# Two graph layers on one core: chunks of 128 edges against windows of 32 nodes, relation products ahead of the gather, and one fused last stage

## The reference, cut to what matters

```python
# layer 0: attention over the edges, 4 heads of 64
enh = x + 0.1 * query_emb
Q, K, V = enh @ Wq + bq, enh @ Wk + bk, enh @ Wv + bv          # [N, 4, 64]
scores = einsum('ehd,ehd->eh', Q[dst], K[src] + 0.2 * rel_w[edge_type_64][:, None]) / 8
w = segment_softmax(scores, dst)
agg = segment_sum(w[:, :, None] * V[src], dst)                 # V itself where a node has no edge
y = layernorm(agg @ Wo + bo + x) * gamma + beta
x = layernorm(x + y)
# layer 1: six relations, then attention of a node's six sums with each other
msgs = (x @ W[r] + b[r])[src]                                  # r = edge_type_6
s = segment_sum(msgs, (dst, r))                                # [N, 6, 256]
q, k, v = split(s @ in_proj_w.T + in_proj_b)
attn = softmax(q k^T / 8) v                                    # 6 x 6, 4 heads
h = (attn @ attn_out_w.T + attn_out_b).mean(over the 6)
x = layernorm(x + (h + x) @ proj_w.T + proj_b)
```

## Time and profile before

| stage | us of the span | TensorE busy | VectorE busy | GpSimd busy | granted clock |
|---|---|---|---|---|---|
| tables | 0 to 230 | 38 | 114 | 60 | 1.00 |
| project | 230 to 427 | 155 | 82 | 66 | 0.96 |
| attend | 427 to 3846 | 2772 | 2895 | 2633 | 0.85 |
| update | 3846 to 4165 | 135 | 168 | 140 | 0.50 |
| relate | 4165 to 7512 | 2047 | 1446 | 1793 | 0.72 |
| mix | 7512 to 9652 | 2069 | 800 | 36 | 0.94 |

### The profile page before, as it was taken

The page is one execution under the profiler, slowest core; times in us unless marked ns, Lnnn a source line. Parts: engine busy times, 40 slices in busy tenths (PEclk is TensorE's granted clock), DMA queues, the critical chain, the costliest instruction groups (busy, mean ns, idle before and its releaser), DMA issues. The chain is left out here.

```text
span 9651.6 us, 171842 instructions
## 1 busy us (share of the span) xinstructions
PE 7214.7 (75%) x38149; PEld 5255.0 (54%) x38149; DVE 5504.5 (57%) x13126; ACT 3186.7 (33%) x13071; POOL 4727.5 (49%) x5036
## 2 busy tenths in 40 slices
PE   1788888888888887446666665666666899999999
PEld 1355555555555554245555555555555566666666
DVE  4488888888888887544444444444444333333333
ACT  0266666666666666100000000000000244433334
POOL 2477777777777776455555555555555000000000
PEclk9888888888888887567777777777777899999989
DMA  2556666666666666233333333333337201111100
GB/s 84 170 184 201 203 203 201 205 202 200 202 202 198 200 201 145 87 95 92 93 92 92 92 90 91 91 95 91 92 93 80 61 28 36 36 36 37 35 27 25
DMA packets 480675, 1131.97 MB, mean 117 GB/s; under 512 B 86354, under 2 KB 280648, under 8 KB 466304
## 3 DMA queue, kind: packets, MB, share of 16 engines
q0 software_dynamic: 233376, 714.12, 26.5%
q1 hardware_dynamic: 221872, 380.98, 11.9%
q10 hardware_dynamic: 25200, 34.03, 1.0%
HBM read 1020.65 MB, written 467.64 MB: 154 GB/s over the span
## 5 line engine op out<-in xcount | busy, mean ns | idle before, releaser
L1401 PE MATMUL re_pa<-re_oh,re_xg 128*128 128x126 f32 x7488 | 1682.2, 364 | 1312.6 <-DVE re_acc L1437 903.8
L1382 POOL DMA_INDIRECT re_xg<-x_rows,re_idx x1872 | 1792.7, 958 | 1545.9 <-PE re_pa L1403 861.8
L689 POOL DMA_INDIRECT at_kv<-kv_rows,at_idx x1760 | 1879.9, 1068 | 695.2 <-issue 494.3
L1437 DVE SCALAR_TENSOR_TENSOR re_acc<-re_acc,re_kp,re_pa 128x378 f32<-128x378 f32 x1872 | 1139.0, 608 | 1879.4 <-remote 789.6
L1401 PEld LDWEIGHTS re_pa<-re_oh,re_xg 128*128 128x128 f32 x7488 | 1411.1, 265 | 1459.1 <-DVE re_acc L1437 1007.5
L859 ACT ACTIVATE at_vs<-at_kv,at_wgt 128x64 f32<-128x64 f32 x7040 | 1725.8, 341 | 75.1 <-DVE at_wgt L947 65.0
L1822 ACT ACTIVATE mx_qk<-mx_pqk,mx_qkv_b 128x504 f32<-128x504 f32 x100 | 68.0, 680 | 4021.3 <-PE mx_pqk L1715 4021.3
L826 PE MATMUL at_p_s<-at_vs,at_eh 128*128 128x264 f32 x3520 | 1074.2, 457 | 225.6 <-DVE at_vs L964 81.9
L826 PEld LDWEIGHTS at_p_s<-at_vs,at_eh 128*128 128x128 f32 x3520 | 753.1, 225 | 471.7 <-issue 218.3
L784 PE MATMUL at_p_r<-g_rel,at_hot 64*128 64x256 bf16 x5280 | 821.7, 295 | 230.8 <-DVE at_kr L904 204.5
L1652 POOL TENSOR_TENSOR mx_xb<-mx_x,mx_proj_b 126x256 f32<-126x256 f32 x50 | 35.2, 725 | 1950.8 <-DMA mx_x<-x_rows 1871.7
(11 more groups left out here) (232 smaller groups left out, 10183.5 us busy)
## 6 DMA issues: line engine op xcount, KB each, us to landing
agg_t<-re_acc SPq DMA_DIRECT2D x936, 189.0 KB
agg_t<-re_acc ACTq DMA_DIRECT2D x936, 189.0 KB
at_hot<-rows SPq DMA_DIRECT2D x110, 1024.0 KB
at_q<-q_rows SPq DMA_DIRECT2D x440, 192.0 KB
sums<-at_acc SPq DMA_DIRECT2D x440, 130.0 KB
mx_agg<-agg_t SPq DMA_DIRECT2D x25, 2268.0 KB
re_xg<-x_rows,re_idx POOLq DMA_INDIRECT x1872
at_kv<-kv_rows,at_idx POOLq DMA_INDIRECT x1760
```

The source lines that it names most:

```text
L689: eng.indirect_dma_start(out=kv[par][:, 4 * c + j, :], out_offset=None, in_=t.kv, in_offset=bass.IndirectOffsetOnAxis(ap=idx[par][:, 4 * c ...
L1382: eng.indirect_dma_start(out=xg[par][:, g, :], out_offset=None, in_=t.x1, in_offset=bass.IndirectOffsetOnAxis(ap=idx[par][:, g:g + 1], axi ...
L1401: eng.matmul(o[:, WR * half:WR * half + WR], xg[par][:, g, P * half:P * half + P], oh[par][:, g, :], start=True, stop=True)
L1437: v.scalar_tensor_tensor(acc[g][:, :], acc[(g - 1) % GS][:, :], kp[par][:, g:g + 1], p_a[g % 4][:, 0:WA], ALU.mult, ALU.add).then_inc(acc_ ...
```

## The change

Nearly every stage is rewritten. The gathers stay indirect DMAs of 128 rows on GpSimd's queue: 1760 in layer 0 and 1875 in layer 1 (1760 and 1872 before).

- **prepare_phase** is tables and project in one block. VectorE and GpSimd make the tables; ScalarE now does every copy of the projection; TensorE does both, table products at written-out places between the 49 tiles (`of_tables`). Layer 0 gets 1760 chunks of 128 edges and 196 windows of 32 nodes, layer 1 windows sorted by size in groups of six (`sort_units`). Also `r0`: each query's product with the 64 relation rows. No bf16 parts of Q.
- **attend_phase** works in 440 groups of four chunks. Keys are turned (8 transposes), and the scores of 128 edges against 32 nodes x 4 heads come from products with the window's queries and with a one-hot of relation and node, which also masks. The maximum is one per row, the sum runs in `acc`. No product is spread to edges, GpSimd only gathers.
- **update_phase** also makes `tx`, the 6 x 256 relation products of each new row, and stores them (39 MB).
- **relate_mix_phase** fuses the last two stages: 316 turns; in turn n the chunks of window n (6.25 of them) are gathered from `tx` and summed, and window n-16 is mixed. The products with the relation matrices and with ones are gone, a window's sums are stored and loaded as rows.
- TensorE multiplies identities (`idle_products`) at the start of update, in the last turns and at the end; in the turns without chunks `gather(v-3)` stands ahead of `weigh(v-2)`.

More of the change, by code:

```diff
@@ L649, in attend_phase @@
+        o_ps = s.sem("o_ps")
         acc_done = s.sem("acc_done")
-        stored = [s.sem(f"stored{i}") for i in range(SUP)]
+        stored = s.sem("stored")
+        cleared = s.sem("cleared")
+        setup = s.sem("setup")
+        why = "prepare_phase writes ends, slots, and counts of loads and stores"
         def run(eng, body):
-            for n in range(4):
-                body(n, n % 2)
-            with eng.Fori(2, NSUP // 2 - 1) as k:
-                body(k * 2, 0)
-                body(k * 2 + 1, 1)
-            for n in range(NSUP - 2, NSUP + 2):
-                body(n, n % 2)
@@ new lines, in ends_of, with ends_and_slots, turn @@
+                def ends_of(w, n):
+                    return nc.values_load_multi_w_load_instructions(
+                        t.ends0[0:1, bass.ds(w, n)], engines=[mybir.EngineType.SP], min_val=1, max_val=K0)[1]
+                def ends_and_slots(w):
+                    return ends_of(w, 4), values(t.slot0, w, 4, ACCS - 1)
+                def turn(w, b):
+                    free = ends_of(w + 3 - RING, 1)[0] if past(w, RING) else None
+                    load(w, b, free)
+                    if past(w, OUT):
+                        ends, slots = ends_and_slots(w - OUT)
+                        for j in range(4):
+                            store(w + j - OUT, ends[j], slots[j])
@@ L1794, in _ @@
-                each(eng, superblock)
-                for j in range(4):
-                    for h in range(H if j < 3 else 0):
-                        weigh(NSB * SBW - 3 + j, SBW - 3 + j, h)
-                    gather(NSB * SBW - 4 + j, SBW - 4 + j)
-                eng.wait_ge(u_done, NSB * SBW)
-                for n, kind, j in nodes_last():
-                    product(NSB, 1, n, kind, j, False, between=0)
+                            mm = eng.matmul(p_sc[e][0:WR, WR * b:WR * b + WR], qk[rows, b, at],
+                                            qk[rows, 2 + b, at], start=False, stop=(b == 1))
@@ L1990 @@
+                eng.wait_ge(acc_zero, 1)
+                eng.wait_ge(tables_in, 16 * TABLES)
+                each(eng, turn)
+                shares(NV - 1, SBW - 1)
+                add_bias(NF - 1)
+                for k in range(3):
+                    take(NF - 1, k)
+                moments(NF - 1)
+                norm(NF - 1)
 class Tensors:
```

2675 lines of the change are left out of this document (1462 added, 1213 removed).

## The result

The changed kernel takes **7159.6 us** (median of four runs, 7142.7 to 7183.5), the kernel before 9534.1 us beside it: ratio 0.7507, 95% interval 0.7489 to 0.7525. That is faster, as forecast, but 5710 us was forecast and 5250 to 6450 the range. The profiled run took 7168.5 us, its span 7166.8.

What follows compares the result with a forecast made beforehand. GpSimd's gather queue was taken to bound the old attend; the new one GpSimd and ScalarE, then GpSimd and TensorE. Prepare 260, attend 2485, update 375, fused 2645 and gaps 15 gave 5780 us, scaled to 5710; range 5250 to 6450.

Steps and rivals of the forecast that it cites:

- Attend, 2485 forecast: Attention stage: 440 groups of four chunks at 5.6 us each, plus 20 us to fill and drain; bounds 2220 and 3190.
- floor: Gathers of both layers, 1760 + 1875 at 1.25 us each: 4544 us, the least the new kernel could take.
- ScalarE's 5.6 us: Attend, per group: 3.6 us of copies and exponentials plus 2 us for 12 register loads per two groups.
- rival 1: Attend: register loads bind at 0.6 us each with nothing beside them, 7.2 us a group, whole 6400 us; chance 0.13.
- Fused, 2645 forecast: Relation sums and mixing: 284 turns at 8.4 us, 2386, plus lead 130, last turns 83, weights 25, end 20.
- the store's ring: Fused stage: the store no longer closes a ring of waits, with 25 slots where eight were; no large store wait.
- the rest is waiting in a ring: Old relate stage: 1.79 us per gather against 1.25 for the queue alone; the difference was put down to engines' waits.
- Rival 2: TensorE binds the fused stage at a clock of 0.85, 9.6 us a turn, whole 6100 us; chance 0.10.
- Rival 3: Gathers stretched by VectorE operations, 0.25 us each: 9.4 us a turn, 6.0 a group, whole 6170 us; chance 0.10.
- Rivals 4 and 5: Rival 4: nothing stalls, 5250 us, chance 0.10; rival 5: TensorE stays at 1.2 GHz, about 10,000 us, chance 0.02.
- they cost nothing there: Fused stage's last 16 turns: identity products fit where TensorE has 4 of 5.2 us; at most 60 us if they miss.
- The scale: Whole kernel: summed span of 5780 us lowered to 5710, as the old span was 1.0126 times its median.

Runs made afterwards that it cites:

- the probe: Changed kernel with stretches appended behind its end: 320 gathers alone, 320 beside 2400 TensorE identity products, products alone; gathers alone went from 1.25 to 1.40 us each.

## Why the prediction was wrong

**Prepare, 260 forecast, 318 measured**, inside its bounds (230 to 330); what took the 58 us was not followed.

**Attend, 2485 forecast, 3201 measured: the step that failed** is the overlap. The prediction gave every engine a sum of its own, "GpSimd: 4 x 1.25 = 5.0 us" among them, and took the longest ("GpSimd and ScalarE are within 0.3 us of each other, so I take 5.6"), as if gathers ran beside the other engines' instructions at no cost to them. The runs show that they don't: the group takes 7.27 us with four gathers, 4.99 with four plain transfers and 4.93 with two gathers and two plain transfers. Its own sign for that, a group of over 6.5 us, came true.

The price of a gather taken alone was wrong too, but that is the smaller part. The 1.25 us of the earlier trace rows is a pace that the probe keeps for 240 us at most; the long run has 1.40. At 1.40 the 3635 gathers are 5089 us, 545 more than the "floor" of 4544, and still less than the 5130 that the two stages were forecast at. What is over in a group, 7.27 - 4 x 1.40 = 1.67 us, is time in which the others catch up (an estimate). Spread over its 183.5 instructions it would be 9 ns each, but no price per instruction holds: 16 fewer saved 17 ns each, 12 more cost 4.5.

Most other terms of the group were right. Four half-width products take 0.22 us, scores and weighing and transposes 4.9 to 5.0 us, the time of the whole group once gathers are gone. VectorE's parts: 0.48, 0.68, 0.74, 0.69, and merges at 0.35. ScalarE's 5.6 us, from which the forecast took its number, was too long: its twelve register loads are three (0.55, 0.48 and 0.48 us for two groups; one fetches eight values), and the group without gathers takes 4.99. So **rival 1 was wrong**, its group time of 7.2 us was met by chance. The signs that it named did come: GpSimd waits for TensorE's weighing (980.2 us, above) and ScalarE's copies on "issue":

```profile
ACT at_own L1029 <- issue: 241.3, 212, 1.4
```

But that wait is as long without the gathers (151.5 us of a stretch of 2000, 152.2 with them), so it isn't what makes the group slow.

**Update, 375 forecast, 350 measured**, at 0.96 of the clock: right.

**Fused, 2645 forecast, 3298 measured: the same step.** "GpSimd and TensorE together, 8.0 each" was again the longer of two queues side by side. TensorE's sum, 7.95 us a turn, was right: between the ends a turn takes 7.75 us without gathers and 10.71 with them, over the 9.2 that was to show the prediction wrong. That the store's ring would be gone was right too; no large wait for a store is in the profile. But the sentence "the rest is waiting in a ring" was the error's other half: I explained relate's 1.79 us for each gather away by its waits. The ring went, and 1.76 stayed. No edit of the kernel before was run, so that 1.79 was the gathers' price there too is argued; its trace agrees: 907 of relate's 3347 microseconds have at most nine instructions, and only 167 of attend's 3419, where GpSimd's merges stand between the gathers. **Rival 2** (a clock of 0.85) found its number, 0.87, but as a consequence; without gathers it is 0.99. **Rival 3** (stretched gathers) fell: 949 ns on average, both stages. **Rivals 4 and 5** fell: no floor at 1.25, no clock at half. Identities and order: "they cost nothing there" fits; whether they earn 20 us is at the edge of what the runs tell.

**The scale.** Dividing 5780 by 1.0126, because the profiled run of before was longer than the others, took off 72 us. The profiled run of the changed kernel is no longer than its others (7166.8 against 7159.6). Of the miss of 1450 us, 1369 are attend and fused, 58 prepare, 72 the scale, less 25 for update and 15 for gaps: 1459, with 7 us between span and median and 2 of rounding.

## What to carry to other kernels

Take an operation's price in a stage from the stage's time divided by its count, also in a stage that "waits", before taking it from its start-to-start distance in a burst; a stage with 1.79 us for each gather and waits in a ring may have the ring's waits from that price. The largest of the engines' sums is a forecast only if the engines don't hold each other up; a run with the suspected operation replaced (4.99 us for 7.27) tells it in one step. Stages full of gathers ran at 1.68 to 1.83 us for each here, and one at 2.46 us for each ran free; what lies between wasn't tried. A cost added to an idle engine in order to measure it must not stand ahead of anything that is waited for, and an edit that takes instructions away may change their form too. Three runs here that were to price an instruction (fewer products, increments on SyncE with and without gathers) each carried such a second effect.

## What the runs showed of the hardware

- An indirect DMA on GpSimd takes the same with half of the bytes (0.95 us), and nearly the same with half of the rows (0.914 us). In an unbroken stream, nothing beside it, it is issued each 1.25 us for 240 us, then each 1.40 us.
- Beside such a stream TensorE gets in one instruction in 1.40 us, 8 us after its start already, and for over 20 us after its end one in 0.7 to 2.1; 50 increments on SyncE take 7.6 us for 2.9. In the kernel a semaphore's increment is recorded 3.3 us after the product that makes it. Plain transfers of the same bytes by GpSimd, 0.54 us each, do nothing of the kind at 251 GB/s.
- It isn't shown what is filled. It is not the transfers, whose first packets keep 1.6 to 1.8 us behind their instruction, nor the number of other instructions: the stopped stretch of the probe has under two a microsecond, the attention stage with plain transfers over 40 in many. The Trainium skill (NOTIFIC — the notification-queue block, Constraints, capacities, measured rates) says that a trace record costs the engine no time and that some 500 records can be held. A store that the gathers fill, that then stops all engines and empties slowly, would look like this. Every run here was traced, so none tells it from another shared path, or whether a run without tracing has the stoppages at all.
- Changing between full and half-width products cost TensorE some 0.17 us each time (an estimate from 0.78 and 0.44 us for a chunk's scores).
- A fill of 0.5 us after every second gather, put into the queue of the engine that seemed to set the pace, made the kernel 2.8% faster.
